# The tail of a cross-attention and soft-mixture kernel: combine logits of the last pair stored slot by slot, and a combine product 336 columns wide

## What is computed

```
x = x + attention(layernorm(x), ctx, Wq, Wk, Wv, Wo)       # per sequence, softmax over 1500 keys
h = layernorm(x)
logits = h @ phi_w.T + phi_b                # (8, 56, 64 experts, 32 slots)
Dm = softmax(logits, over slots)            # "dispatch"
C  = softmax(logits, over experts)          # "combine"
Xt = einsum('tznp,tzd->npd', Dm, h)         # all 448 tokens feed 2048 slots
Xt = tanh(normalise(clip(Xt)))              # mean and variance over the 128 features
Yt = einsum('npd,ndH->npH', Xt, expert_w) + expert_b
y  = einsum('tznp,npH->tzH', C, Yt)
out = x + y
```

## Time and profile before

| | us |
|---|---|
| median of 3 runs | 433.64 |
| lowest, highest | 432.48, 433.64 |
| the profiled execution | 433.6 |
| its span in the trace | 431.7 |
| TensorE busy in it | 422.8 (98%) |
| VectorE, ScalarE, GpSimd busy | 333.9, 245.2, 167.7 |

### The profile page before, as it was taken

One profiled execution on the slowest core, in us unless ns is written; L12 is line 12 of the kernel. 1 busy time (PEld: TensorE's weight loads), 2 busy tenths in 40 slices (PEclk: granted clock), 3 DMA queues, 4 the chain that ended last, 5 costly groups with the idle time before them and its releaser, 6 DMA issues.

```text
span 431.7 us, 7476 instructions
## 1 busy us (share of the span) xinstructions
PE 422.8 (98%) x3004; PEld 388.5 (90%) x3004; DVE 333.9 (77%) x612; ACT 245.2 (57%) x412; POOL 167.7 (39%) x98
## 2 busy tenths in 40 slices
PE   7999999999999999999999999999999999999897
PEld 5898999999999999889999998899999898999887
DVE  3788756875786778767898689978988899669981
ACT  2576647665664546654673766466655564644641
POOL 6409800524050405032608053617146443456710
DMA  7401110213020011110120012101000010296000
GB/s 203 143 16 14 33 58 14 57 44 100 14 53 33 20 14 22 64 18 14 14 73 20 12 14 72 20 12 15 2 18 14 0 14 18 53 260 176 2 2 23
DMA packets 15418, 19.05 MB, mean 44 GB/s; under 512 B 4032, under 2 KB 10960, under 8 KB 15384
## 3 DMA queue, kind: packets, MB, share of 16 engines
q1 hardware_dynamic: 15384, 18.58, 17.3%
HBM read 18.32 MB, written 0.26 MB: 43 GB/s over the span
## 4 chain that ended last, share of the span: by engine, by line
PE 82%; DVE 11%; ACT 5%; DMA 1%; issue 0%; SPq 0%; ACTq 0%
PE turned L736 16%; PE acc L756 8%; PE acc L757 8%; PE acc L758 8%; PE scores L720 8%; PE scores L726 8%; PE scores L723 8%; PE misc L773 3%; PE misc L642 2%; DVE pT_l L1424 2%; ACT prob L1170 2%; DVE small L1414 2%; PE scores L1100 2%; PE misc L800 2%; ACT logit L1221 1%; ACT pT_h L1163 1%
## 5 line engine op out<-in xcount | busy, mean ns | idle before, releaser
L1163 ACT CAST pT_h<-turned 125x512 fp32r<-125x512 f32 x168 | 95.3, 591 | 124.1 <-PE turned L736 123.5
L1424 DVE TENSOR_TENSOR pT_l<-turned,pT_h 125x512 fp32r<-125x512 f32 x168 | 112.3, 686 | 60.2 <-ACT pT_h L1163 59.5
L1414 DVE TENSOR_REDUCE small<-scores 128x1 f32<-128x500 f32 x168 | 108.1, 674 | 4.4 <-PE scores L726 4.1
L736 PE MATMUL turned<-ident,prob 128*125 128x128 f32 x672 | 94.6, 276 | 1.9 <-DVE pT_l L1424 1.6
L736 PEld LDWEIGHTS turned<-ident,prob 128*125 128x125 f32 x672 | 87.5, 187 | 9.5 <-DVE pT_l L1424 3.5
L756 PE MATMUL acc<-pT_h,ctx_nh 125*128 125x256 f32 (+1 forms) x288 | 94.1, 327 | 0.0
L1170 ACT ACTIVATE prob<-scores,small 128x1500 f32<-128x1500 f32 x56 | 85.0, 1518 | 10.2 <-DVE small L1417 9.8
L758 PE MATMUL acc<-pT_h,ctx_nl 125*128 125x256 f32 (+1 forms) x288 | 86.5, 300 | 0.0
L757 PE MATMUL acc<-pT_l,ctx_nh 125*128 125x256 f32 (+1 forms) x288 | 86.3, 300 | 0.0
L720 PE MATMUL scores<-ctx_th,qk_h 128*128 128x500 f32 x168 | 67.7, 403 | 0.4 <-ACT prob L1170 0.4
L726 PE MATMUL scores<-ctx_th,qk_l 128*128 128x500 f32 x168 | 65.3, 389 | 0.0
(11 more groups left out here) (216 smaller groups left out, 567.8 us busy)
## 6 DMA issues: line engine op xcount, KB each, us to landing
ctx_raw<-in_ctx_dram SPq DMA_DIRECT2D x7, 750.0 KB
rbc<-rden_row SPq DMA_DIRECT2D x15, 128.0 KB, 3.3
rbc<-rden_row SPq DMA_DIRECT2D x8, 192.0 KB, 3.2
eb<-in_L_ffn_expert_b_dram SPq DMA_DIRECT2D x4, 256.0 KB, 5.6
ctx_raw<-in_ctx_dram SPq DMA_DIRECT2D x3, 224.0 KB, 4.9
wq_sb<-in_L_xattn_Wq_dram SPq DMA_DIRECT2D x2, 256.0 KB, 4.6
wk_sb<-in_L_xattn_Wk_dram SPq DMA_DIRECT2D x2, 256.0 KB, 5.2
wv_sb<-in_L_xattn_Wv_dram SPq DMA_DIRECT2D x1, 512.0 KB, 3.7
```

The costliest lines, as they stand in the source:

```text
L736: last = tr(turned[0:CK, m, 128 * c:128 * c + 128], prob[u][:, CK * j:CK * j + CK], ident[:, :])
L1163: nc.scalar.copy(pT_h[0:CK, PLACES[g // NT % 2][t], CPB * k:CPB * k + CPB, :], turned[0:CK, (KB * u + k) % 2, :].rearrange("p (c r) -> p c ...
L1414: m = v.tensor_reduce(bankmax[:, u, k:k + 1], scores[:, k, 0:KW], AX.X, ALU.max)
L1424: v.tensor_tensor(pT_l[0:CK, place, dst, :], turned[0:CK, (KB * u + k) % 2, :].rearrange("p (c r) -> p c r", c=CPB), pT_h[0:CK, place, dst ...
```

## The change

1. **Layout of the last pair's combine logits.** `copy_logits(3, c)` writes slot by slot: the 64 experts of one slot are adjacent, and the copy's elements land 64 words (256 bytes) apart. Maximum and sum over experts then read adjacent elements, and the sum is one instruction in place of two halves and a join. The two shifts work on runs of 32 adjacent elements, with one value of `cmax` for each run. The exponential works on the same 2048 columns as before.
2. **Scale.** `last_combine_scale(r)` reads with a step of 64 words and writes expert by expert into `disp[3]`, whose dispatch weights are used up by then. `turn_comb(LAST)` reads from there.
3. **Order on VectorE.** `add_expert_bias(0)` now stands ahead of the upper shift.
4. **Combine of the first three pairs.** `combine(r)` holds `yt[:, k, :]` as weights (128 x 128) and streams 336 columns of `combT`: four products per round in place of 12. The result is transposed, [128 features, 336 tokens], in bank S0. ScalarE copies it to a new tile `y2T`, TensorE turns it back with three transposes into bank M1 (`turn_y2`), and VectorE adds `x` from there.
5. **Order on TensorE.** `combine(1)` follows `combine(0)` directly, ahead of `turn_xt(2)`; `turn_y2` stands between the last pair's rounds 1 and 2.

```diff
-            def combine_shift_upper(q):
+            def last_combine_shift_upper():
-                half_n = slice(N_EXP // 2, N_EXP)
-                dve.wait_ge(cmax_dve, q + 1)
-                v.tensor_tensor(by_expert(comb[q][:, :])[:, half_n, :], by_expert(logit[q][:, :])[:, half_n, :],
-                                cmax[q][:, :].unsqueeze(1).broadcast_to([PT, N_EXP // 2, P_SLOT]),
+                part = slot_rows(comb[LAST][:, :])[:, :, N_EXP // 2:N_EXP]
+                dve.wait_ge(cmax_dve, LAST + 1)
+                v.tensor_tensor(part, part, cmax[LAST][:, :].unsqueeze(2).broadcast_to([PT, P_SLOT, N_EXP // 2]),
                                 ALU.subtract).then_inc(csub_dve, 1)
...
+                    dst = logit[q][:, :].rearrange("p (s n) -> p n s", n=N_EXP)[:, EPB * c:EPB * c + EPB, :]
+                    src = bank(LOGIT_BANKS[q][c])[0:PT, :].rearrange("p (n s) -> p n s", s=P_SLOT)
+                    nc.scalar.copy(dst, src).then_inc(logit_act, 1)
...
+            def last_combine_max():
+                dve.wait_ge(logit_act, LC * (LAST + 1))
+                v.tensor_reduce(cmax[LAST][:, :], slot_rows(logit[LAST][:, :]), AX.X, ALU.max).then_inc(cmax_dve, 1)
...
+            def last_combine_sum():
+                dve.wait_ge(cexp_act, LAST + 1)
+                v.tensor_reduce(csum[LAST][:, :], slot_rows(comb[LAST][:, :]), AX.X, ALU.add).then_inc(csum_dve, 1)
+                dve.wait_ge(csum_dve, LAST + 1)
+                v.reciprocal(csum[LAST][:, :], csum[LAST][:, :]).then_inc(crec_dve, 1)
...
+            def last_combine_scale(r):
+                dve.wait_ge(crec_dve, LAST + 1)
+                src = comb[LAST][:, :].rearrange("p (s n) -> p n s", n=N_EXP)[:, EPB * r:EPB * r + EPB, :]
+                v.tensor_tensor(by_expert(comb_by_expert[LAST][:, QUARTER * r:QUARTER * r + QUARTER]), src,
+                                csum[LAST][:, :].unsqueeze(1).broadcast_to([PT, EPB, P_SLOT]),
                                 ALU.mult).then_inc(comb_dve, 1)
...
+            def combine(r):
+                pe.wait_ge(yt_dve, r + 1)
                 for k in range(4 * r, 4 * r + 4):
-                    for q in range(q0, q1):
-                        last = mm(bank(SLOT_BANKS[part])[0:PT, H * (q - q0):H * (q - q0) + H],
-                                  combT[:, k, PT * q:PT * q + PT], yt[:, k, :],
-                                  start=(k == 0 and q == q0), stop=(k == NS - 1), skip_group_check=True)
+                    last = mm(bank(S0)[:, 0:LAST * PT], yt[:, k, :], combT[:, k, 0:LAST * PT],
+                              start=(k == 0), stop=(k == NS - 1))
...
+            def turn_y2():
+                pe.wait_ge(y2T_act, 1)
+                for q in range(LAST):
+                    last = tr(bank(M1)[0:PT, D * q:D * q + D], y2T[:, PT * q:PT * q + PT], ident[:, :])
+                last.then_inc(y2turn_pe, 1)
...
+            act.wait_ge(y2_pe, 1)
+            nc.scalar.copy(y2T[:, :], bank(S0)[:, 0:LAST * PT]).then_inc(y2T_act, 1)
```

More of the change, by code:

```diff
@@ L197, in xattn_softmoe_kernel @@
         comb = logit
+        comb_by_expert = [comb[0], comb[1], comb[2], disp[3]]
         stats_at = [stat0_at, stat1_at, t0_at + KB8, t0_at + KB8 + 384]
@@ L209, in xattn_softmoe_kernel @@
         yt = at("yt", [128, NS, H], F32, t0_at)
+        y2T = at("y2T", [D, (PAIRS - 1) * PT], F32, xnT_at)
         out_sb = at("out_sb", [PT, NQ, D], F32, oT_at + 2048)
@@ L333, in xattn_softmoe_kernel @@
         y2_pe = sem("y2_pe")
+        y2T_act = sem("y2T_act")
+        y2turn_pe = sem("y2turn_pe")
         out_dve = sem("out_dve")
@@ L623, in _ @@
             slot_root(1)
-            combine_shift(LAST, 0, N_EXP // 2)
+            last_combine_shift_lower()
             slot_root(2)
@@ L1028, in turn_comb @@
                         k = 4 * r + c
-                        last = tr(bank(RING[r])[:, PT * c:PT * c + PT], comb[q][:, 128 * k:128 * k + 128],
+                        last = tr(bank(RING[r])[:, PT * c:PT * c + PT], comb_by_expert[q][:, 128 * k:128 * k + 128],
                                   ident[0:PT, 0:PT])
@@ L1092, in experts, with combine_last @@
                 last.then_inc(yt_pe, 1)
-            def combine(part, r):
-                pe.wait_ge(yt_dve, max(r, part) + 1)
-                q0, q1 = PARTS[part]
+            def combine(r):
+                pe.wait_ge(yt_dve, r + 1)
                 for k in range(4 * r, 4 * r + 4):
-                    for q in range(q0, q1):
-                        last = mm(bank(SLOT_BANKS[part])[0:PT, H * (q - q0):H * (q - q0) + H],
-                                  combT[:, k, PT * q:PT * q + PT], yt[:, k, :],
-                                  start=(k == 0 and q == q0), stop=(k == NS - 1), skip_group_check=True)
+                    last = mm(bank(S0)[:, 0:LAST * PT], yt[:, k, :], combT[:, k, 0:LAST * PT],
+                              start=(k == 0), stop=(k == NS - 1))
                 if r == 3:
                     last.then_inc(y2_pe, 1)
+            def combine_last(r):
+                pe.wait_ge(combT_act, 12 + r + 1)
+                for k in range(4 * r, 4 * r + 4):
+                    last = mm(bank(ACC)[0:PT, 0:H], combT[:, k, LAST * PT:TOK], yt[:, k, :],
+                              start=(k == 0), stop=(k == NS - 1))
+                if r == 3:
+                    last.then_inc(y2_pe, 1)
+            def turn_y2():
[3 more added lines that the diff above has]
+                last.then_inc(y2turn_pe, 1)
             pe.wait_ge(ew_in, 16)
@@ L1110, in _ @@
             experts(1)
-            combine(0, 0)
+            combine(0)
+            combine(1)
             turn_xt(2)
-            combine(0, 1)
             experts(2)
             turn_xt(3)
-            combine(0, 2)
+            combine(2)
             experts(3)
             turn_comb(LAST)
[L1119 to L1122, removed]
+            combine(3)
+            combine_last(0)
+            combine_last(1)
+            turn_y2()
+            combine_last(2)
+            combine_last(3)
         @block.scalar
```

41 lines of the change are left out of this document (21 added, 20 removed).

## The result

The changed kernel takes 432.24 us against 433.46 us of the kernel before, medians of 20 runs each; the ratio is 0.9973, with a 95% interval of 0.996 to 0.9986. It is faster by 1.2 us. That is clear of the noise, but at 0.27% a little short of the 0.3% at which I had drawn the border between faster and the same. The forecast was 432.2. Single executions far outside the rest, one of 2370 us here and one of 697 us in `t1_changed_again`, are left out of the ratios and their intervals.

What follows compares the result with a forecast made beforehand. The late exponential, through tanh 2 and turn_xt(2), and TensorE's work after it were taken as the bound. Profiled 433.6, span 431.7, less 1.45 us gave span 430.25 and time 432.2, range 431.4 to 433.2.

Steps and rivals of the forecast that it cites:

- The exponential comes later: On ScalarE, the last pair's combine exponential begins at 409.62, 0.7 us later than before, following VectorE's upper shift.
- The wide product: In the combine of the first three pairs, eight records of 336 columns take 2.25 us, 0.37 less a round.
- Rounds 0 and 1, and who holds `turn_xt(2)`: On TensorE, combine(1) ends at 413.0, just ahead of turn_xt(2) at 413.24, so both rounds are hidden.
- The list behind it: TensorE from turn_xt(2) on: combine(3) starts at 421.59, the last add at 427.87 instead of 429.33, gaining 1.45 us.
- The strided scale: VectorE's last-pair scale takes 0.95 us a quarter instead of 0.62, and costs nothing up to 1.14.
- my rival: VectorE's last-pair scale: the 64-word step costs 1.3 us a quarter, 432.8, or at 2.50 ns 433.0; chance 0.09.
- The sum is no gain: VectorE's sum over experts saves some 1.8 us ahead of bias 2, which waits for experts(2), so no gain.
- Stores, `y2T`: At the end, stores land 2.2 and 1.6 us after issue; the y2T copy takes under 0.59 and costs nothing.
- The price of the store rival: Final stores: the second queues behind the first, landed at 428.9, then 0.7 us more, giving 432.9; chance 0.07.

Runs made afterwards that it cites:

- t1_changed_again: The changed kernel itself, unaltered, timed once more: 432.13 us, ratio 0.997 to the kernel before, tail (first dispatch maximum of the last pair to last add) 38.85 us.
- e11_old_layout: The changed kernel's wide combine products and both new orders, on the layout of before: tail 39.24 us, against 38.85 in the changed kernel.
- e7_three_of_112: The changed kernel with each 336-column combine product cut in three of 112, weights still yt: tail 40.31 us, against 38.85 in the changed kernel.
- e3_shift_first: The changed kernel with the upper shift put back ahead of bias 0 on VectorE: tail 38.68 us, against 38.85 in the changed kernel.

## Why the prediction was right, point by point

- **The exponential comes later.** Right: 20.60 us after the mark, where 409.62 - 389.12 = 20.50 was forecast. Maximum 2.25 (2.27), idle 2.02 (1.9), upper shift 1.22 (1.20). GpSimd's half took 1.91 in place of 2.37 and was long done, so the shift did not wait for it, and the 1.70 of the row was not met. `e11_old_layout` takes the layout out of the question: its upper shift, on the old layout but clear of GpSimd's half, takes 1.22 too.
- **The wide product.** Right in size: 421.33 to 423.61 is 2.28, 416.38 to 418.73 is 2.35 with its handover, against 2.25 and 2.35. The reason that I gave, time by columns, holds for the old record and for the wide one. It does not hold for the three cut records of `e7_three_of_112`, which the prediction had not looked at, and which I then expected at 0.10 us each instead of 0.112. The gain needs both, fewer columns and wide records.
- **Rounds 0 and 1, and who holds `turn_xt(2)`.** Right: tanh does. Tanh 2 ends 24.05 us after the mark, and with the 0.14 us that lay between the two before (410.85 + 1.55 in the earlier trace rows to 412.54 in the earlier trace rows) it lets `turn_xt(2)` go at 24.19; the trace has it at 24.20. TensorE's own work would have reached it at 19.43 + 4.62 = 24.05: the two rounds take 4.62 us where nothing holds them (`e3_shift_first`), and not the 4.5 of my sum. So the two are closer than I had it, 0.15 us apart and not 0.24. The 0.08 us against the forecast of 24.12 are the exponential's 0.10, less 0.02 that my sum had too much, since it added 0.7 for 0.68.
- **The list behind it.** Gaps of 0.68 and 0.55 us ahead of `experts(2)` and `turn_xt(3)`, as expected; transposes 0.33 (425.35 to 425.68), as taken; tail 38.85 against 38.75. Every start from `turn_xt(2)` to the last add lies 0.07 to 0.11 us behind the forecast, so most of the miss of 0.10 is there at `turn_xt(2)`.
- **The strided scale.** Right: 0.98 us a quarter (0.95), and 1.14 as the point from which it costs. The strided reductions give a fixed part of 0.09 (two of 1024 elements at 1.90 less one of 2048 at 3.71, `e11_old_layout`). With that off, 0.98 is 1.7 ns an element at a step of 64 words. The 1.73 ns for one hopping source of the Trainium skill ("Vector Engine (DVE) Microarchitecture Reference", section 5.2) agrees with it. Its 2.50 ns is stated for both sources or the output stepping by 24 words; here one source alone steps, so my rival had taken it beyond its condition, and no run here tests it.
- **The sum is no gain.** Wrong, and hidden by the right total. I had compared it with the time at which bias 2 is due in the new list, but did not ask what the old sum would have done there: `e11_old_layout` puts it at 0.39 us. The whole was right because the forecast ran the new sum through the list.
- **Stores, `y2T`.** Right: 2.2 and 1.6 us. The price of the store rival, 0.7 us, did not follow from its own numbers: queued, the second store would have landed at 428.9 + 0.7 = 429.6, ahead of its own 428.2 + 1.6 = 429.8. And the copy of 336 columns took 0.44 and was done 1.1 us before it was needed.

The chance of 0.48 for faster and 0.45 for the same was fair: the tail gained 1.36 us, 0.31%, and the medians moved by 1.2.

## What to carry to other kernels

Walk each engine's list with the times of the trace and write down what is last at every handover. A saving ahead of an in-order wait is lost in the wait (the faster maximum, 1.46 us, worth nothing), and one behind it may pay only after another edit has moved the due time (the sum, 0.39 us); two edits worth +0.78 and -0.55 alone gave -1.36 together.

When an engine idles for its input and another waits behind it, try the orders together: two moves that gave 0.17 us less and 1.41 us more by themselves gave, with a third, 1.0 us less.

In float32, count streamed columns for each choice of which operand is held as weights, and then check that the records are wide enough for the columns to set their time: here 336 columns were, and 112 over weights of 128 columns were not. The fewer columns can pay even at the price of transposing the result back. A weight-load row that is busy all the time does not tell the two cases apart, since it was so in both.

## What was not expected of the hardware

- With float32 weights of 128 columns a record takes 0.112 us whether 112 columns are streamed or 128. With 128 columns over weights of 112 columns it takes 0.109.
- Before the change VectorE's shift was stretched beside GpSimd's half (1.70 us for 1.22). In `e3_shift_first` it is the other way round: beside VectorE's shift of 1.24 us, GpSimd's operation on four columns took 1.09, where it takes 0.23 otherwise, and it ended 0.09 us after the shift.

```profile
404.74 1.24 DVE L1707 TENSOR_TENSOR logit<-logit,cmax 112x1024 f32<-112x1024 f32 x1
```

```profile
404.98 1.09 POOL L570 TENSOR_SCALAR xt_nb<-xt_mv 128x4 f32<-128x4 f32 x1
...
410.35 0.23 POOL L570 TENSOR_SCALAR xt_nb<-xt_mv 128x4 f32<-128x4 f32 x1 [2.59 <-DVE xt_mv L1695]
```

- GpSimd's subtraction of 1024 elements takes 1.91 us in the new layout, where its second operand stays the same over runs of 32, and 2.37 in the old one, where it changes with every element. Which feature of the layout does it was not tested; VectorE beside it does not, since `e11_old_layout` has 2.38 without the shift alongside.
- The time ahead of the mark varies by 3.1 us (387.59 to 390.68) over the fourteen profiles of twelve kernels, all with the same code there. Where it goes was not looked into. Differences of single runs below that say nothing, while the tail repeats within 0.01 us.
